# Unread identity products on the matrix engine at four places of a four-layer cross-attention kernel

## The chip, the cores and the metric

The kernel runs on one core of one Trainium2 chip. The metric is the device time of one execution, in microseconds. The engines are PE (TensorE, the matrix engine; its weight loads are listed as PEld), DVE (VectorE), ACT (ScalarE), POOL (GpSimd) and SP (SyncE, which here only issues transfers).

## The reference

Four layers are applied to `x` (16 sequences of 56 tokens, width 256), each with a context of 1,500 keys of width 128 per sequence. Cut to what is computed:

```python
# layer 0, one head over the context, then a gate and a norm
mp = ctx @ W_mem;  a = softmax(x @ mp.T / 16);  mc = a @ mp
x = rmsnorm(x + sigmoid(concat(x, mc) @ W_gate.T + b) * mc)
# layers 1 and 3: 16 heads of 64 over the context, then a feed-forward network
q = layernorm(x) @ Wq / 8;  k, v = split(ctx @ Wkv)
x = x + tanh(g1) * (softmax(mask(q @ k.T)) @ v) @ Wo
x = x + tanh(g2) * gelu(layernorm(x) @ W1) @ W2
# layer 2: causal self-attention with rotary positions (two sets of weights, picked
# per token), then 16 heads of 8 over the context, then a gated MLP
x = x + where(vm, self_attn(rmsnorm(x)) @ v_dense, ... @ l_dense)
x = x + softmax(cq @ ck.T) @ cv @ cdense_w
x = x + where(vm, mlp_v(rmsnorm(x)), mlp_l(rmsnorm(x)))
```

## The kernel before, in words

The program is one hand-ordered instruction list per engine. Engines meet through semaphores: `then_inc` signals, `on.wait_ge` waits and is left out where an earlier wait of the same engine already covers it. PE writes its products into eight PSUM banks; a product of one stage takes the next bank in turn, and `bank_free` waits until that bank's last content was emptied by ACT or DVE. The 896 tokens are 7 tiles of 128, handled as tiles 0 to 3 and 4 to 6 where a norm is computed. An fp32 product is recorded as two MATMUL instructions, a transpose as one; a transpose streams the identity (`ident`) through PE with the data as weights.

Four stages matter here.

- **First attention** (`pe_l0`, layer 0). Eight units of two sequences. Step `s` on PE does the scores of unit `s` (L666), the sums of unit `s-2` (L678, 24 products of 64 columns) and the transposes of the softmax of unit `s-1` (L692, 12 of them), in that order. ACT and DVE copy the transposes out (L702) before the sums of that unit can start. Steps 8 and 9 have no scores left. Then all engines meet (`join`), `pe_l0_gate` makes the 7 products of L768, the 4 of L772 and the 28 of L778, and POOL, after cutting the next query weights (L562, L564), multiplies and adds per tile (L796, L798) for DVE's square sums (L812).
- **First norm** (`pe_transposes` L502 and `pe_queries`). DVE computes two norms in a row for tiles 0 to 3 (from L819 on), PE transposes the rows, ACT scales them out (L557), DVE cuts them into two parts (L562, L564), and the projections of layer 1 start (L582, fp32r, 6 products each; then L875). DVE goes on with the norms of tiles 4 to 6 before it empties the first projection (L618).
- **Self-attention** (`pe_front`). Eight pairs of sequences. Step `s` does, in this order, the turn of tile `s-1` (L1451), queries and keys of tile `s` (L1431), values of pair `s` (L1443), the transposed weights of pair `s-2` (L1474), the scores of pair `s-1` (L1466), the sums of pair `s-2` (L1485) and the output product of tile `s-4` (L1495). From step 7 on tiles are used up, and from step 8 on pairs too, so the work of PE thins out. The weights of a pair wait for DVE's softmax, whose last operation is L1619; it starts from the scores (L1602). Then come a norm (L502) and the queries of the next attention (L1532).
- **Third attention** (`pe_narrow`). 96 slots of scores, and seven slots behind them without scores. Slots 97 to 99 hold only the 12 `fill` calls of the last group of rows, four transposes each (L1799), into two banks in turn, which ACT (L1903) and DVE (L1901) copy out. Then the last sums (L1812), the norm's transposes (L502) and the MLP (L2062).

## Time and profile before

| | |
|---|---|
| runs, us | 2384.64, 2389.21, 4637.36 (median 2389.21) |
| profiled execution, its own time | 2383.55 us |
| its span | 2381.8 us |
| mean granted clock of PE | 0.983 |
| PE busy | 2299.6 us (97% of the span) |
| DVE busy | 1576.9 us (66%) |
| ACT busy | 1289.9 us (54%) |
| POOL busy | 669.4 us (28%) |

One of the three runs, 4637.36 us, is far from the other two and from the profiled execution. The granted clock is a share of PE's full 2.4 GHz: 1.00 is that level, 0.50 is 1.2 GHz, and a value between them in a row means that the stretch holds both. The parts of the profile used below are the share of the chain that ended last, windows (busy time of each engine and the granted clock in chosen stretches) and timelines (instructions in order of time, neighbours of one kind merged; the bracket at the end is the idle time before it and what ended it).

### The profile page before, as it was taken

What the parts mean: (1) busy time and instruction counts of PE and PEld (TensorE: products, weight loads), DVE (VectorE), ACT (ScalarE), POOL (GpSimd) and SP (SyncE); (2) the same over time, 40 slices, a digit from 0 to 9 for tenths busy, and PEclk for the clock granted to TensorE, in tenths of its full rate; (3) what the DMA queues carried; (4) which work ended last, traced back from release to release, by engine and by line L of the source; (5) the groups of instructions that cost most, each with busy time, mean ns of one, the idle gap of its engine ahead of it and who ended that gap; (6) DMA issues with size and microseconds to landing.
All of it is one profiled execution on the core that took longest, in us unless ns stands there. A gap on an engine that the chain in (4) does not pass through costs nothing.

```text
span 2381.8 us, 42122 instructions
## 1 busy us (share of the span) xinstructions
PE 2299.6 (97%) x16416; PEld 1900.5 (80%) x16416; DVE 1576.9 (66%) x4256; ACT 1289.9 (54%) x2204; POOL 669.4 (28%) x752
## 2 busy tenths in 40 slices
PE   6979999999999999789999999999999999999999
PEld 3857999999999895456666666556899999999988
DVE  2256777777777656677777777414777777777764
ACT  1235555555555543267777777412555555555553
POOL 0045343444443224210000000011543434344330
PEclk8889999999999999899999999899999999999999
DMA  8720111111211110010000000310021111111010
GB/s 264 201 93 17 46 43 46 43 48 41 58 31 43 55 36 21 1 53 27 27 27 27 27 14 1 127 36 4 19 58 40 50 45 44 46 43 46 27 54 17
DMA packets 36136, 116.02 MB, mean 49 GB/s; under 512 B 4618, under 2 KB 18546, under 8 KB 35938
## 3 DMA queue, kind: packets, MB, share of 16 engines
q1 hardware_dynamic: 33474, 101.04, 14.0%
q10 hardware_dynamic: 2464, 12.29, 2.0%
q8 instruction: 131, 2.15, 0.4%
q14 instruction: 67, 0.55, 0.1%
HBM read 112.40 MB, written 0.92 MB: 48 GB/s over the span
## 4 chain that ended last, share of the span: by engine, by line
PE 90%; ACT 5%; DVE 3%; DMA 1%; issue 0%; ACTq 0%; SPq 0%; DVEq 0%
PE bank L1051 20%; PE bank L1038 19%; PE bank L1065 12%; PE bank L1799 7%; PE bank L582 7%; PE bank L2062 3%; PE bank L1812 3%; PE bank L1785 3%; ACT n_scores L1911 3%; PE bank L678 2%; PE bank L1759 2%; PE bank L2075 2%; PE bank L875 1%; PE bank L1763 1%; PE bank L1232 1%; PE bank L1077 1%
## 5 line engine op out<-in xcount | busy, mean ns | idle before, releaser
L1101 ACT CAST p_T_high<-bank 125x512 fp32r<-125x512 f32 x672 | 350.6, 595 | 515.9 <-PE bank L1065 515.9
L1158 DVE TENSOR_TENSOR p_T_low<-bank,p_T_high 125x512 fp32r<-125x512 f32 x672 | 422.5, 684 | 258.0 <-ACT p_T_high L1101 258.0
L1124 DVE CUSTOM_DVE_ANT_0 scores<-bank,mask 128x500 f32<-128x500 f32 x672 | 418.4, 672 | 0.8 <-PE bank L1038 0.8
L1111 ACT ACTIVATE scores<-scores,row_max 128x1500 f32<-128x1500 f32 x224 | 353.4, 1578 | 2.7 <-DVE row_max L1129 2.7
L1051 PE MATMUL bank<-p_T_high,keys_nat_high 125*128 125x256 f32 (+1 forms) x1152 | 346.0, 300 | 1.7 <-ACT inverse L1108 1.7
L1051 PE MATMUL bank<-p_T_high,keys_nat_low 125*128 125x256 f32 (+1 forms) x1152 | 346.3, 301 | 0.0
L1051 PE MATMUL bank<-p_T_low,keys_nat_high 125*128 125x256 f32 (+1 forms) x1152 | 346.2, 301 | 0.0
L1065 PE MATMUL bank<-ident,scores 128*125 128x128 f32 x2688 | 331.1, 273 | 2.7 <-ACT scores L1111 2.7
L1065 PEld LDWEIGHTS bank<-ident,scores 128*125 128x125 f32 x2688 | 318.2, 187 | 5.7 <-ACT scores L1111 5.7
L1038 PE MATMUL bank<-keys_T_high,q_stage_high 128*128 128x500 f32 x672 | 280.1, 417 | 0.0
L1946 DVE CUSTOM_DVE_ANT_0 n_scores<-bank,n_zeros 112x500 f32<-112x500 f32 x384 | 236.9, 673 | 56.7 <-PE bank L1785 56.7
L1038 PE MATMUL bank<-keys_T_high,q_stage_low 128*128 128x500 f32 x672 | 261.2, 389 | 0.0
L1038 PE MATMUL bank<-keys_T_low,q_stage_high 128*128 128x500 f32 x672 | 260.7, 388 | 0.0
L1799 PEld LDWEIGHTS bank<-ident,n_scores 112*125 112x125 f32 x1536 | 186.9, 190 | 88.1 <-issue 29.7
L1799 PE MATMUL bank<-ident,n_scores 112*125 112x112 f32 x1536 | 220.2, 287 | 13.4 <-ACT n_p_T L1903 7.3
L1051 PEld LDWEIGHTS bank<-p_T_high,keys_nat_high 125*128 125x128 f32 x1152 | 216.7, 188 | 10.2 <-ACT inverse L1108 2.2
L1051 PEld LDWEIGHTS bank<-p_T_low,keys_nat_high 125*128 125x128 f32 x1152 | 217.0, 188 | 8.5
L1051 PEld LDWEIGHTS bank<-p_T_high,keys_nat_low 125*128 125x128 f32 x1152 | 216.7, 188 | 0.0
L1911 ACT ACTIVATE n_scores<-n_scores,n_stats 112x1500 f32<-112x1500 f32 x128 | 197.8, 1546 | 0.4 <-DVE n_stats L1952 0.4
L1164 POOL CAST q_stage_high<-q_and_o 128x256 fp32r<-128x256 f32 (+1 forms) x96 | 41.7, 434 | 412.8 <-PE bank L1038 412.6
L1038 PEld LDWEIGHTS bank<-keys_T_high,q_stage_low 128*128 128x128 f32 x672 | 126.2, 188 | 26.3
L1038 PEld LDWEIGHTS bank<-keys_T_high,q_stage_high 128*128 128x128 f32 x672 | 126.9, 189 | 19.0 <-issue 1.6
(242 smaller groups left out, 3611.9 us busy)
## 6 DMA issues: line engine op xcount, KB each, us to landing
ctx_T<-in_ctxT SPq DMA_DIRECT2D x32, 750.0 KB, 4.3
ctx_nat<-in_ctx SPq DMA_DIRECT2D x32, 672.0 KB
q_and_o<-in_ctxT SPq DMA_DIRECT2D x16, 750.0 KB, 9.2
n_ctx_T<-in_ctxT SPq DMA_DIRECT2D x16, 750.0 KB, 4.2
q_and_o<-in_ctx ACTq DMA_DIRECT2D x16, 672.0 KB
mask_bytes<-in_mask SPq DMA_DIRECT2D x32, 187.5 KB, 5.2
weights<-in_L_W SPq DMA_DIRECT2D x4, 1024.0 KB, 6.2
ctx_nat<-in_ctx SPq DMA_DIRECT2D x32, 78.0 KB
```

What stands on the lines that cost most here:

```text
L582: x = e.matmul(out, left[i], right[j], start=start and n == 0, stop=stop and n == 2)
L1038: m = e.matmul(psum[c][:, 0:CHK], QSs[i][g % 2][:, lo:lo + 128], KTs[j][b % 2][:, cols], start=(n == 0), stop=(n == 2))
L1051: m = e.matmul(psum[6 + g % 2][:, cols_g], KNs[i][b % 2][0:KP, cols], PTs[j][g % 2][0:KP, k, cols_g], start=(k == 0 and n == 0), stop=(k = ...
L1065: m = e.transpose(psum[3 + c][0:KP, 128 * k:128 * k + 128], SB[u % 2][:, (4 * c + k) * KP:(4 * c + k + 1) * KP], ident)
L1101: e.copy(PTs[0][g % 2][0:KP, 4 * c:4 * c + 4, lo:lo + 128], psum[3 + c][0:KP, :].rearrange("p (k r) -> p k r", k=4)).then_inc(s_eh, 1)
L1111: e.activation(SB[s % 2], SB[s % 2], ACT.Exp, bias=mx[:, s % 4, 3:4], accum_out=mx[:, s % 4, 4:5]).then_inc(s_ex, 1)
L1124: e.tensor_tensor_reduce(out=SB[u % 2][:, c * CHK:(c + 1) * CHK], in0=psum[c][:, 0:CHK], in1=mb[:, c * CHK:(c + 1) * CHK], scale=1.0, scal ...
L1158: e.tensor_tensor(low, psum[3 + c][0:KP, :].rearrange("p (k r) -> p k r", k=4), high.bitcast(F32), ALU.subtract).then_inc(s_el, 1)
L1785: return e.matmul(psum[r][0:PAIR, 0:CHK], n_qs[i][b % 2][rows, PAIR * hh:PAIR * hh + PAIR], CK[j][b % 2][rows, c * CHK:(c + 1) * CHK], sta ...
L1799: m = e.transpose(psum[4 + t % 2][0:KP, PAIR * k:PAIR * k + PAIR], n_unit(quad, r)[0:PAIR, at:at + KP], ident[0:PAIR, 0:PAIR])
L1911: e.activation(unit, unit, ACT.Exp, bias=n_st[0:PAIR, quad % 2, r, 3:4], accum_out=n_st[0:PAIR, quad % 2, r, 4:5]).then_inc(s_n_ex, 1)
L1946: e.tensor_tensor_reduce(out=n_unit(quad, r)[0:PAIR, c * CHK:(c + 1) * CHK], in0=psum[r][0:PAIR, 0:CHK], in1=n_zeros[0:PAIR, :], scale=1.0 ...
```

## The change

A new helper, `pe_fill_in`, multiplies the identity by itself, repeated side by side: 512 columns wide, or 256 with `copies=2`, in plain fp32. It signals nothing, and no engine reads the result. It is called at five spots:

1. In steps 8 and 9 of the first attention, two and one products, ahead of the sums.
2. Ahead of the first transposes of layer 1's norm, eight products, and ahead of the first projection, two.
3. In steps 7, 8 and 9 of the self-attention, two, four and four products, ahead of the pair's transposed weights.
4. In slots 97 to 99 of the third attention, one product of 256 columns behind each `fill`.

DVE, ACT, POOL and SP keep their lists as they were. The waits that come with the products make sure that the bank they write into is free.

```diff
--- before.py
+++ after.py
@@ -494,6 +494,13 @@
                 on.wait_ge(*prod.emptied[prod.ahead[i]])
 
 
+        def pe_fill_in(e, at_bank, times, copies=4):
+
+            for _ in range(times):
+                e.matmul(at_bank[:, 0:128 * copies].rearrange("p (o n) -> p o n", o=copies), ident,
+                         ident.rearrange("p (o n) -> p o n", o=1).to_broadcast([128, copies, 128]),
+                         start=True, stop=True)
+
         def pe_transposes(e, on, n, h):
             for (m, k), i in n.parts[h].items():
                 bank_free(on, i)
@@ -666,6 +673,9 @@
                             x = e.matmul(psum[c][64 * n:64 * n + 64, 0:CHK], q0T_flat[:, PAD * b:PAD * b + PAD],
                                          kt0[b % 4][:, c * CHK:(c + 1) * CHK], start=True, stop=True)
                         x.then_inc(s_sc, 1)
+                if s >= L0U:
+                    on.wait_ge(s_mx, 3 * L0U)
+                    pe_fill_in(e, psum[0], L0U + 2 - s)
                 if s >= 2:
                     u = s - 2
                     on.wait_ge(s_l0_ea, 2 * u + 2)
@@ -1507,6 +1517,9 @@
                     values(s)
                 if s == 0:
                     pe_transposes(e, on, in_norm, 1)
+                if NT <= s < PAIRS + 2:
+                    on.wait_ge(s_rot, 3 * NT)
+                    pe_fill_in(e, front_bank(F_QK), (2, 4, 4)[s - NT])
                 if 2 <= s < PAIRS + 2:
                     weights(s - 2)
                 if 1 <= s <= PAIRS:
@@ -1841,8 +1854,11 @@
                         pe_cd(e, on, t)
                 for half in range(2):
                     if 0 <= quad < QUADS:
-                        fill(quad, ts[2 * half])
-                        fill(quad, ts[2 * half + 1])
+                        for t in ts[2 * half:2 * half + 2]:
+                            fill(quad, t)
+                            if s > SLOTS:
+                                on.wait_ge(*prod.emptied[cd_prod[0]])
+                                pe_fill_in(e, bank(cd_prod[0]), 1, 2)
                     if made:
                         product(*made[half])
                     if b < B:
@@ -2153,7 +2169,11 @@
             pe_q0(e, on)
             pe_l0(e, on)
             pe_l0_gate(e, on)
+            bank_free(on, g1.q_norm.parts[0][0, 0])
+            pe_fill_in(e, bank(g1.q_norm.parts[0][0, 0]), 8)
             pe_transposes(e, on, g1.q_norm, 0)
+            bank_free(on, g1.q[0, 0])
+            pe_fill_in(e, bank(g1.q[0, 0]), 2)
             pe_queries(e, on, g1)
             pe_cross(e, on, layers[0], g1)
             join(e, on, J["l1"])
```

PE at the end of the first attention, steps 8 and 9, before. The names are those of the program: `area` holds the scores, `q_and_o` the keys; the bracket lists the semaphores waited for.

```order
L692 MATMUL bank<-ident,area 125x128 x11
L678 MATMUL bank<-area,q_and_o 128x64 [waits s_o_out,s_l0_keys0,s_l0_evac_dve,s_l0_evac_act]
L678 MATMUL bank<-area,q_and_o 128x64 x11
L678 MATMUL bank<-area,q_and_o 128x64 [waits s_l0_keys1]
L678 MATMUL bank<-area,q_and_o 128x64 x11
L692 MATMUL bank<-ident,area 125x128 [waits s_l0_normed]
L692 MATMUL bank<-ident,area 125x128 x11
L678 MATMUL bank<-area,q_and_o 128x64 [waits s_o_out,s_l0_keys2,s_l0_evac_dve,s_l0_evac_act]
```

And now:

```order
L702 MATMUL bank<-ident,area 125x128 x11
L500 MATMUL bank<-ident 128x512 [waits s_max]
L500 MATMUL bank<-ident 128x512
L688 MATMUL bank<-area,q_and_o 128x64 [waits s_o_out,s_l0_keys0,s_l0_evac_dve,s_l0_evac_act]
L688 MATMUL bank<-area,q_and_o 128x64 x11
L688 MATMUL bank<-area,q_and_o 128x64 [waits s_l0_keys1]
L688 MATMUL bank<-area,q_and_o 128x64 x11
L702 MATMUL bank<-ident,area 125x128 [waits s_l0_normed]
L702 MATMUL bank<-ident,area 125x128 x11
L500 MATMUL bank<-ident 128x512
L688 MATMUL bank<-area,q_and_o 128x64 [waits s_o_out,s_l0_keys2,s_l0_evac_dve,s_l0_evac_act]
```

Two products stand between the transposes and the first sums, one between the next transposes and the last sums; nothing else moved.

PE around the first norm, now; `x_normed` holds the rows to be transposed, `x_T_r` the cut ones. Before, the rows of L500 were not there, and the wait for `s_emptied_dve` stood at the first projection.

```order
L788 MATMUL bank<-weights,x_T 128x256 x15
L500 MATMUL bank<-ident 128x512 x8
L509 MATMUL bank<-ident,x_normed 128x128 [waits s_rows] x4
L509 MATMUL bank<-ident,x_normed 128x128 [waits s_emptied_dve]
L509 MATMUL bank<-ident,x_normed 128x128 x3
L500 MATMUL bank<-ident 128x512 [waits s_emptied_dve]
L500 MATMUL bank<-ident 128x512
L589 MATMUL bank<-x_T_r,weights_r 128x448 [waits s_cut,s_w_l1a,s_weights_cut,s_emptied_act]
```

The eight follow the last gate product without a wait; the other two wait only for a bank that DVE emptied in the gate stage.

PE at slot 97 of the third attention, now; `n_scores` are the softmax rows.

```order
L1825 MATMUL bank<-n_p_T,q_and_o 32x224 x8
L1812 MATMUL bank<-ident,n_scores 125x112 [waits s_n_p_act,s_n_exp]
L1812 MATMUL bank<-ident,n_scores 125x112 x3
L500 MATMUL bank<-ident 128x256 [waits s_emptied_dve]
L1812 MATMUL bank<-ident,n_scores 125x112 [waits s_n_p_dve]
L1812 MATMUL bank<-ident,n_scores 125x112 x3
L500 MATMUL bank<-ident 128x256
L1812 MATMUL bank<-ident,n_scores 125x112 [waits s_n_p_act]
```

Before, the groups of four transposes followed each other directly; now each of the 12 has a product behind it. The first of them waits for the residual of tile 0, for which its bank was last used.

## Rows read from the trace of the kernel before

**Rows 1.** The page, part 4: the chain that ended last, by engine.

```profile
PE 90%; ACT 5%; DVE 3%; DMA 1%; issue 0%; ACTq 0%; SPq 0%; DVEq 0%
```

**Rows 2.** Windows. Stretch, length, busy us (instructions) per engine, PEclk, DMA share, GB/s.

```profile
97.70:108.00 10.30, 10.30 (x50) 10.30 (x50) 0.28 (x1) 0.89 (x2) 0.00 (x0) 0.50 0.52 133
108.00:111.40 3.40, 2.57 (x24) 2.41 (x23) 0.69 (x1) 0.28 (x1) 0.00 (x0) 1.00 0.00 0
111.40:121.60 10.20, 9.79 (x39) 8.88 (x39) 1.55 (x4) 0.20 (x1) 0.00 (x0) 0.50 0.24 74
...
142.10:155.80 13.70, 5.58 (x17) 4.44 (x18) 12.19 (x38) 1.97 (x4) 0.33 (x1) 0.50 0.00 0
...
975.00:978.40 3.40, 3.33 (x12) 2.10 (x14) 0.01 (x1) 1.07 (x2) 3.40 (x4) 0.50 0.02 5
...
1497.20:1510.80 13.60, 12.61 (x74) 10.09 (x74) 5.59 (x20) 8.72 (x16) 0.00 (x0) 0.50 0.67 237
```

**Rows 3.** Timeline, PE, 84 to 142. Start, us, engine, line, idle before it.

```profile
87.87 5.57 PE L678 MATMUL bank<-area,q_and_o 125*128 125x64 f32 x48
93.28 1.53 PE L692 MATMUL bank<-ident,area 128*125 128x128 f32 x12
96.47 9.38 PE L678 MATMUL bank<-area,q_and_o 125*128 125x64 f32 x48 [1.67 <-ACT area L702]
105.65 2.66 PE L692 MATMUL bank<-ident,area 128*125 128x128 f32 x12
109.14 8.44 PE L678 MATMUL bank<-area,q_and_o 125*128 125x64 f32 x48 [0.83 <-ACT area L702]
117.98 5.07 PE L768 MATMUL bank<-weights,q_and_o 128*128 128x256 f32 x14 [0.41 <-DVEq L331]
...
126.79 12.32 PE L778 MATMUL bank<-weights,x_T 128*128 128x256 f32 x56 [0.72 <-ACT x_T L616]
```

**Rows 4.** Timelines, POOL and DVE, of the gate stage.

```profile
131.07 0.73 POOL L796 TENSOR_TENSOR area<-area 128x256 f32<-128x256 f32 x1
...
139.49 0.68 DVE L819 TENSOR_SCALAR row_stats<-row_stats 128x4 f32<-128x4 f32 x1
```

**Rows 5.** Timeline, PE, 144 to 168: first norm and first projections.

```profile
147.69 2.30 PE L502 MATMUL bank<-ident,x_normed 128*128 128x128 f32 x8 [8.58 <-DVE x_normed L524]
152.52 4.16 PE L582 MATMUL bank<-x_T_r,weights_r 128*128 128x448 f32 x12 [2.53 <-DVE x_T_r L564]
158.45 1.02 PE L875 MATMUL bank<-area,weights 64*128 64x448 f32 x4 [1.77 <-DVE area L618]
```

**Rows 6.** Timeline, PE, 954 to 1050: last self-attention pairs.

```profile
964.80 1.09 PE L1474 MATMUL bank<-ident,q_and_o 128*128 128x128 f32 x8
965.83 1.73 PE L1466 MATMUL bank<-q_and_o 128*64 128x448 f32 x8
...
975.07 1.97 PE L1474 MATMUL bank<-ident,q_and_o 128*128 128x128 f32 x8 [2.74 <-DVE q_and_o L1619]
...
986.67 1.97 PE L1474 MATMUL bank<-ident,q_and_o 128*128 128x128 f32 x8 [4.86 <-DVE q_and_o L1619]
988.56 3.26 PE L1466 MATMUL bank<-q_and_o 128*64 128x448 f32 x8
...
1012.98 3.19 PE L1532 MATMUL bank<-x_T,weights 128*128 128x448 f32 x4 [1.01 <-DVE x_T L541]
```

**Rows 7.** Timeline, PE, 1486 to 1517: end of the third attention.

```profile
1495.42 3.09 PE L1799 MATMUL bank<-ident,n_scores 112*125 112x112 f32 x16 [1.72 <-ACT q_and_o L1903]
1498.78 5.75 PE L1799 MATMUL bank<-ident,n_scores 112*125 112x112 f32 x24 [0.27 <-ACT q_and_o L1903]
1505.25 3.22 PE L1812 MATMUL bank<-q_and_o,n_values 125*32 125x224 f32 x32 [0.72 <-DVE q_and_o L1901]
...
1508.54 3.04 PE L502 MATMUL bank<-ident,area 128*128 128x128 f32 x16
1511.51 1.72 PE L1812 MATMUL bank<-q_and_o,n_values 125*32 125x224 f32 x32
```

## The prediction

> **What bounds the kernel now.** I read four views, in this order. The chain of waits first: 90% of the chain that ended last is PE [rows 1]. So a microsecond counts where PE works on the chain, and a wait of PE counts only for what it does to the work behind it. Next the windows, cut where the granted clock changes: PE runs at its low level, 1.2 GHz, in 97.7 to 108.0 and 111.4 to 121.6 (end of the first attention and start of the gate), 142.1 to 155.8 (first norm), a few short stretches from 975 on (last self-attention pairs), and 1497.2 to 1510.8 (end of the third attention) [rows 2]. Each of them comes behind a place where PE waited. These are the five spots of the edit. Third, the timelines of PE there, for what the same instruction takes at either level: 48 instructions of sums take 5.57 us at the high level and 9.38 or 8.44 us at the low one; 12 transposes 1.53 and 2.66 [rows 3]. Last, the other engines there, to see who would be late next.
>
> **What a new product costs.** The 28 gate products of 256 columns, 56 instructions, take 12.32 us at the high level [rows 3]: 0.44 us each. A new product of 512 columns is then 0.88 us, one of 256 columns 0.44 us. At the low level it is twice that: 1.76 and 0.88 us. All of it is PE time; no other engine's list changes, and the new waits are on work long done (the last score maxima, a bank emptied in the gate stage, the last rotation), so I cost them at nothing. The one with something close behind it is the bank of tile 0's residual in slot 97; DVE empties it in the pause that ACT leaves there anyway.
>
> **First attention.** Two products, 1.76 us, stand in a wait of 1.67 us [rows 3]: 0.1 us lost. If the clock stays up, the sums behind them fall from 9.38 to 5.57 us: 3.8 us won. From the start of the next transposes (105.65) to the last sums (109.14) it is 3.49 us. The same distance at the high level is 3.19 us, from 93.28 to 96.47, so at least 0.3 us is won; but there ACT issues key transfers before it copies, which step 9 doesn't. At most the transposes' own 1.13 us is won. I take 1.1, nearer the place itself, since the third product (0.88 us) then just fills the 0.83 us of wait. The last sums: 8.44 to 5.57, 2.9 us. The seven products of L768: 5.07 us against 7 x 0.44 = 3.1, 2.0 us. Not all of that counts. POOL starts the tiles at 131.07, behind its cut of weights whose transfer is issued at the join, so relative to the join it moves not at all [rows 4]. Four tiles at two operations of 0.73 us bring it to about 137, and DVE's square sum and two adds to about 138.3, where it starts the norm at 139.49 today [rows 4]: 1.2 us. Sum: 3.8 + 1.1 + 2.9 + 1.2 - 0.1 = **8.9 us**.
>
> **First norm.** Eight products, 7.0 us, in a wait of 8.58 us; two, 1.8 us, in one of 2.53 us [rows 5]. They cost nothing at the high level. What do they bring? Very little: the transposes wait for DVE's rows, and the 12 projections (4.16 us, mostly low) are followed by a wait for DVE [rows 5], which meanwhile works through the norms of tiles 4 to 6. Faster projections only make the wait of 1.77 us longer, to about 3 us. That wait has no product in it, and it is as long as the one of 2.74 us behind which the clock fell at 975 [rows 2, 6]. From there PE is the bound. A low stretch of 3.4 us, the length in [rows 2], can cost half of that, 1.7 us; two of them 3.4. Between +0.2 (transposes a little earlier) and -3.4 I take **-1.0 us**: one such stretch, more likely than not.
>
> **Last self-attention pairs.** The waits of 2.74 and 4.86 us [rows 6], and a third like the second, get 1.8, 3.5 and 3.5 us of products: hidden. DVE's softmax between them is not shortened, but it starts when PE's transposes and scores are done, so their low clock is on the chain. Second pair: transposes 1.97 against 1.09, scores 3.26 against 1.73 [rows 6]: 2.4 us. First pair: transposes 0.9, of the scores only the beginning is low (the low stretch is 3.4 us long, which caps the gain at 1.7): 1.5 us. Third: its transposes, 0.9, and those of the norm behind them, in part waiting for rows: 1.1, between 0.9 and 1.7. The queries at 1012.98 take 3.19 us, half of it too much [rows 6]; but the small waits ahead of them, 1.01 us the last, stay uncovered, so I take half of 1.6: 0.8. Sum: **5.8 us** (4.5 to 6.7).
>
> **End of the third attention.** Here the products are partly on the chain. The last 24 transposes, six groups, take 5.75 us at the low level, 0.96 us a group [rows 7]. At the high level 12 transposes take 1.53 us [rows 3], so four with 112 columns about 0.4, and the product 0.44: 0.84 a group. 6 x 0.12 = 0.7 us won. Ahead of them ACT's exponentials and copies set the pace (waits of 1.72 and 0.27 us [rows 7]). Then the sums, 3.22 against 1.72 us: 1.5. The norm's 16 transposes, 3.04 us, would take about 2.0: 1.0. Sum: **3.2 us**. If the clock were not low here anyway, the 12 products, 5.3 us, less the waits of 1.72, 0.27 and 0.72, would cost 2.6 us.
>
> **A rule against it.** PE's clock rose at 108.0 [rows 2], and from 105.65 on it had done nothing but 12 transposes, 2.66 us long [rows 3]; they stream the same identity that the new products stream. On the other side 24 transposes from 1498.78 did not raise it [rows 2, 7]. The Trainium skill says in "TensorE: Matmul & The Clock Gate", Part 4 (PE-mode transpose), that in transpose mode the full clock doesn't engage, since it doesn't count as PE being busy in the same way. By that rule the products between transposes have to hold the clock alone. By the first of the two rows the transposes help them; I go by it, and keep the other as a rival.
>
> **The sum.** 8.9 - 1.0 + 5.8 + 3.2 = 16.9 us, against the profiled execution's own 2383.55 us: 2366.6 us. The two runs shown near it are 1.1 and 5.7 us above that execution, so I put the median of the changed kernel 1.9 us higher: **2368.5 us**, 0.9% below the median of 2389.21.
>
> **The rivals.**
> - *Given back (chance 0.22).* The clock falls in waits that no product covers, above all behind the first projections (-3.4), the queries stay slow (5.0 instead of 5.8), and at the end of the third attention the typical execution has little low clock to win back, so that the products show (-2.6). 8.9 - 3.4 + 5.0 - 2.6 = 7.9 us: 2375.7, with the same 1.9 on top 2377.6. For it: clock falls come behind waits of quite different length, so they may not be the same in each execution. Against: the waits with products are the longest ones.
> - *Transposes don't count (0.07).* The end of the third attention stays low: 12 products at 0.88 = 10.6 us less 2.7 of waits cost 7.9 us instead of a gain of 3.2. 16.9 - 11.1 = 5.8 us: 2377.8 us. The rule above is the Trainium skill's form of it. The rise at 108.0 speaks against it.
> - *Slower than before (0.05).* The products don't hold the clock (a product that is mostly zeros is not counted, or too little), and so run at 1.76 us each. They outgrow the waits: 3.5 - 1.7 and 1.8 - 0.8 in the first attention, 14.1 - 8.6 and 3.5 - 2.5 at the norm, 3.5 - 2.7 and twice 7.0 - 4.9 at the pairs, 7.9 at the third attention: 22 us, 2406 us. The eight ahead of the norm decide it: from 8.58 / 8 = 1.07 us each on they delay it. Against: identity was streamed up to 108.0, and the clock rose.
> - *Forecast (0.66).* All four places keep the high clock, 2361 to 2374 us.
>
> **The numbers.** The time is the forecast's. The range goes from 2360 us (first attention 9, pairs 6.7, third attention 4, norm +0.2, and executions like the profiled one) to 2381 us, which takes in both rivals at 2378 and a median like the slower of the two runs. About 1 in 8 is left out, mostly the slower case. All cases lie within 2% of 2389.21 (2341 to 2437), about what a measurement of this kernel can tell from no change: 0.98 within, 0.01 on either side.
>
> **What would show it.** Windows of the changed kernel: clock 1.00 through the first attention's end and the gate, the sums 5.6 us each, the join 7.7 us earlier; DVE's norm start about 9 us earlier; the wait ahead of the products of L875 about 3 us, and perhaps a low stretch behind it; the distance between two pairs' transposes 10.3 us, as from 964.80 to 975.07, instead of 11.6 [rows 6]; groups of 0.84 us in slots 98 and 99, sums of 1.7 us behind them. The forecast is wrong if a product takes 1.76 us in one of the waits, if the copies of step 9 still take 3.2 us, or if sums follow with the clock at 0.50 all the same.

## The result

The changed kernel takes **2376.77 us** (median, 2369.47 to 2382.78), the kernel before 2385.01 us in the same comparison: ratio 0.9966, 95% interval 0.9954 to 0.9978, that is 8 us less (5 to 11). Measured again on the chip of the last mends, beside 2384.66 us of before, it took 2372.58 us: 0.9952 (0.9935 to 0.9969), 11 us less. Over all 22 executions its median is 2375.9 us. The direction, the range and the class (within 2%) were forecast; the gain was put at 16.9 us, and half to two thirds of it came.

The profiled execution of the changed kernel has a time of 2373.76 us and a span of 2372.0 us, 9.8 us less than before. Its windows, cut where the granted clock changes (columns as in [rows 2]), show what was promised and one thing that was not:

```profile
98.40:105.20 6.80, 6.80 (x33) 6.80 (x33) 0.27 (x1) 0.74 (x2) 0.00 (x0) 0.50 0.28 80
105.20:142.70 37.50, 34.10 (x157) 24.76 (x156) 16.56 (x49) 9.13 (x18) 16.88 (x18) 1.00 0.47 143
142.70:146.10 3.40, 3.40 (x6) 1.19 (x5) 2.82 (x9) 1.14 (x3) 0.00 (x0) 0.50 0.00 0
969.60:1002.90 33.30, 27.15 (x187) 13.33 (x188) 22.40 (x46) 7.85 (x14) 4.30 (x5) 1.00 0.00 0
1030.20:1043.90 13.70, 13.70 (x77) 10.66 (x76) 7.09 (x21) 8.70 (x15) 1.59 (x3) 0.50 0.00 1
1480.20:1506.60 26.40, 25.30 (x251) 19.68 (x250) 11.37 (x34) 15.46 (x28) 0.00 (x0) 1.00 0.47 162
```

Against [rows 2], the pairs (969.60) and the end of the third attention (1480.20) are now without any low clock. But the clock is still at 0.50 from 98.40, though for 6.8 us instead of 10.3; again at 142.70; and, new, for 13.7 us from 1030.20 on, inside the third attention. Before had there only the short low stretch (a stretch with the clock at 0.50) that begins 9.2 us into that stage, and the changed kernel has one like it, 3.4 us from 1016.5 on. The row of before:

```profile
1026.20:1029.60 3.40, 3.40 (x12) 1.33 (x5) 2.48 (x8) 0.52 (x1) 0.00 (x0) 0.50 0.00 0
```

The timeline of PE at the end of the first attention (start, us, instruction, idle before it) answers [rows 3]:

```profile
92.42 1.88 PE L500 MATMUL bank<-ident 128*128 128x512 f32 x4
94.25 2.89 PE L688 MATMUL bank<-area,q_and_o 125*128 125x64 f32 x24
98.06 5.14 PE L688 MATMUL bank<-area,q_and_o 125*128 125x64 f32 x24 [0.92 <-DMA q_and_o<-in_ctx]
103.00 2.60 PE L702 MATMUL bank<-ident,area 128*125 128x128 f32 x12
105.43 1.02 PE L500 MATMUL bank<-ident 128*128 128x512 f32 x2
106.42 5.54 PE L688 MATMUL bank<-area,q_and_o 125*128 125x64 f32 x48
112.38 3.29 PE L778 MATMUL bank<-weights,q_and_o 128*128 128x256 f32 x14 [0.41 <-DVEq L331]
```

The two products (92.42) fill the wait for ACT as planned, 1.88 us in four instructions. Half-way through unit 6's sums PE then waits 0.92 us, but for DMA: the keys. The clock falls right behind it, at 98.40; the second 24 sums take 5.14 us, the first 24 took 2.89, and the transposes take 2.60 (2.66 in [rows 3]). From these transposes to the last sums it is 3.42 us, hardly less than the 3.49 of before. Only the last sums (106.42) are as forecast, 5.54 us instead of 8.44. The gate starts at 112.38, 5.6 us earlier, where 7.7 were expected.

The first norm, for [rows 5]:

```profile
131.56 7.03 PE L500 MATMUL bank<-ident 128*128 128x512 f32 x16
140.85 1.74 PE L509 MATMUL bank<-ident,x_normed 128*128 128x128 f32 x8 [2.26 <-DVE x_normed L531]
142.42 3.32 PE L500 MATMUL bank<-ident 128*128 128x512 f32 x4
145.58 2.94 PE L589 MATMUL bank<-x_T_r,weights_r 128*128 128x448 f32 x12
151.47 1.02 PE L885 MATMUL bank<-area,weights 64*128 64x448 f32 x4 [2.95 <-DVE area L625]
152.42 2.16 PE L589 MATMUL bank<-x_T_r,weights_r 128*128 128x448 f32 x6
154.51 1.87 PE L885 MATMUL bank<-area,weights 64*128 64x448 f32 x4
156.31 1.51 PE L589 MATMUL bank<-x_T_r,weights_r 128*128 128x448 f32 x6
```

Eight products take 7.03 us: 0.88 us each, the price of the forecast. The two behind the transposes take 3.32 us, 1.66 each, for the clock is low there, from 142.70 on. It costs nothing here: from the transposes to the projections it is 4.73 us, against 4.83 in [rows 5]. The wait ahead of L885 (L875 before) grew from 1.77 to 2.95 us, as forecast, and part of what follows is low: 2.16 us for six projections that take 1.51 at 156.31.

The pairs and queries, for [rows 6], and the place of the new loss, on PE:

```profile
969.59 1.09 PE L1484 MATMUL bank<-ident,q_and_o 128*128 128x128 f32 x8 [0.83 <-DVE q_and_o L1632]
970.61 1.72 PE L1476 MATMUL bank<-q_and_o 128*64 128x448 f32 x8
...
974.61 3.60 PE L500 MATMUL bank<-ident 128*128 128x512 f32 x8
979.63 1.09 PE L1484 MATMUL bank<-ident,q_and_o 128*128 128x128 f32 x8 [1.42 <-DVE q_and_o L1632]
...
989.68 1.09 PE L1484 MATMUL bank<-ident,q_and_o 128*128 128x128 f32 x8 [1.42 <-DVE q_and_o L1632]
...
1002.55 3.00 PE L1545 MATMUL bank<-x_T,weights 128*128 128x448 f32 x4 [1.01 <-DVE x_T L548]
1006.31 2.78 PE L1772 MATMUL bank<-n_ctx_T,value_weights 128*128 128x500 f32 x6 [0.77 <-DVEq L331]
```

```profile
1029.95 1.82 PE L1812 MATMUL bank<-ident,n_scores 112*125 112x112 f32 x8 [1.60 <-ACT n_p_T L1919]
```

From pair to pair it is 10.04 us, 10.3 were forecast, and scores take 1.72 us. The queries at 1002.55 are still slow, 3.00 us. In slot 4 of the third attention PE waits 1.60 us for ACT's copies of the transposed weights, and the low 13.7 us start there.

The end of the third attention, for [rows 7]:

```profile
1488.69 0.69 PE L1812 MATMUL bank<-ident,n_scores 112*125 112x112 f32 x4 [0.83 <-ACT q_and_o L1919]
...
1492.28 0.59 PE L1812 MATMUL bank<-ident,n_scores 112*125 112x112 f32 x4
...
1493.15 0.59 PE L1812 MATMUL bank<-ident,n_scores 112*125 112x112 f32 x4
...
1497.95 1.72 PE L1825 MATMUL bank<-q_and_o,n_values 125*32 125x224 f32 x32 [0.27 <-DVE q_and_o L1917]
...
1499.70 2.03 PE L509 MATMUL bank<-ident,area 128*128 128x128 f32 x16
...
1506.60 3.65 PE L2078 MATMUL bank<-x_T,weights 128*128 128x448 f32 x9
```

A group takes 0.87 us (1492.28 to 1493.15), 0.84 forecast; sums 1.72 and the norm's transposes 2.03 us, as forecast.

**Where the microseconds are.** One execution says little about a clock that falls at different waits each time. So here are means over the profiles of three executions of before and four of the changed kernel, between the same instructions on PE (us):

```
stretch                               step said   before  changed  gained
start to sums of unit 6                  -0.1      96.1     95.3     0.9
sums of unit 6 to sums of unit 7         +4.9      13.2     13.0     0.2
sums of unit 7 to the gate's first       +2.9      10.2      6.0     4.2
gate to first absorbed queries           +1.2      40.7     39.2     1.5
from there to the first pair             -1.0     764.5    766.3    -1.8
first five pairs                          0        52.1     52.1     0.0
last three pairs, norm, queries          +5.8      41.4     36.5     5.0
third attention up to its last slots      0       471.7    475.4    -3.7
end of the third attention               +3.2      29.3     26.4     3.0
the rest                                  0       865.4    865.4     0.0
sum                                      16.9    2384.7   2375.6     9.1
```

Two lines hold the missing 8 us: the sums of unit 6, and the third attention.

### The profile page after: what moved, and what is told of

Read it like the earlier page. It is cut to its first block, busy times and chain, and to the rows that moved or that the text cites. A ratio compares the mean times of both kernels' runs of the same rounds, so it can differ in the third digit from the quotient of the medians.

```text
span 2372.0 us, 42261 instructions
## 1 busy us (share of the span) xinstructions
PE 2309.4 (97%) x16486; PEld 1901.8 (80%) x16486; DVE 1576.2 (66%) x4256; ACT 1288.7 (54%) x2204; POOL 668.8 (28%) x752
## 3 DMA queue, kind: packets, MB, share of 16 engines
q8 instruction: 132, 2.16, 0.4%
## 4 chain that ended last, share of the span: by engine, by line
PE 89%; ACT 5%; DVE 3%; DMA 2%; POOL 0%; issue 0%; ACTq 0%; SPq 0%; DVEq 0%; POOLq 0%
PE bank L1061 20%; PE bank L1048 19%; PE bank L1075 12%; PE bank L1812 8%; PE bank L589 7%; PE bank L2078 3%; PE bank L1825 3%; PE bank L1798 3%; ACT n_scores L1927 2%; PE bank L1772 2%; PE bank L2091 2%; PE bank L688 2%; PE bank L885 1%; PE bank L1776 1%; PE bank L1242 1%; PE bank L1087 1%
## 5 line engine op out<-in xcount | busy, mean ns | idle before, releaser
L1061 PEld LDWEIGHTS bank<-p_T_high,keys_nat_high 125*128 125x128 f32 x1152 | 216.7, 188 | 10.2 <-ACT inverse L1118 2.2
```

The lines of the kernel that those rows point to most:

```text
L1061: m = e.matmul(psum[6 + g % 2][:, cols_g], KNs[i][b % 2][0:KP, cols], PTs[j][g % 2][0:KP, k, cols_g], start=(k == 0 and n == 0), stop=(k = ...
```

## The experiments

**One piece at a time.** Each kernel is the changed one with three of its four pieces taken out; for example the one that keeps the first attention:

```diff
-                if NT <= s < PAIRS + 2:
-                    on.wait_ge(s_rot, 3 * NT)
-                    pe_fill_in(e, front_bank(F_QK), (2, 4, 4)[s - NT])
...
-                            if s > SLOTS:
-                                on.wait_ge(*prod.emptied[cd_prod[0]])
-                                pe_fill_in(e, bank(cd_prod[0]), 1, 2)
...
-            pe_fill_in(e, bank(g1.q_norm.parts[0][0, 0]), 8)
...
-            pe_fill_in(e, bank(g1.q[0, 0]), 2)
```

> Only the three products at the end of the first attention stay. Theory 1 (the profiled execution of before had more low clock than a usual one, so the sum was made too large): 4 to 7 us faster than before; the sums behind the first two products partly wait for keys that are still in transfer. Rival (the sizes by place were right, and the gain is lost again in low stretches elsewhere that the change brings): 8.9 us faster, and the granted clock of the profile is 1.00 from 94 us to the join.

> Only the ten products around the first norm stay. Both theories: 0 to 2 us slower than before, no gain. The norm's chain on VectorE is as long as before, the wait behind the first 12 projections grows from 1.8 to about 3 us, and in most executions the clock falls behind it. If instead it is 2 us or more faster, the projections' low clock was on the chain and my step was wrong.

> Only the ten products at the last self-attention pairs stay. Theory 1: 4 to 5 us faster, from the distances between the transposes of two pairs (10.0 us each in place of 11.6 and 12.4). Rival: 5.8 us faster in the stretch. Both: at least as much as the other places together, if theory 1 holds.

> Only the twelve products at the end of the third attention stay. Theory 1: within 1 us of before, since a usual execution of before has less low clock there and the products themselves stand on the chain (12 x 0.44 us less the waits). Rival: 3.2 us faster, as the two profiles show it (3.1 us).

Measured, as ratios to before: first attention alone 0.9982 (0.9972 to 0.9993), 4.3 us; norm alone 1.0001 (0.9991 to 1.001), nothing; pairs alone 0.9981 (0.9971 to 0.9991), 4.5 us; end of the third attention alone 0.998 (0.997 to 0.9991), 4.8 us. The first three came as their theories said. The pieces add up to 13.6 us, each with some 2.5 us of uncertainty; that this is more than the 8 to 11 us that they give together is likely, but not clear of these errors. For the third attention the rival was right: from the first products behind it to the next stage it takes 28.9 to 29.6 us in the six executions without the products, and 26.3 to 26.4 in every one with them. The kernel with the pairs alone gives the pairs' 5 us in full (35.5 us instead of 41.4) and loses them: its third attention takes 475.2 us instead of 469.8.

The profiled execution of the first piece alone was the fastest of its eleven (2370.85 us against a median of 2380.18): its keys came in time and its sums took 7.8 us. In the one with the end of the third attention alone they didn't (PE; start, us, instruction, idle):

```profile
96.80 4.06 PE L685 MATMUL bank<-area,q_and_o 125*128 125x64 f32 x24 [1.98 <-DMA q_and_o<-in_ctx]
101.94 5.39 PE L685 MATMUL bank<-area,q_and_o 125*128 125x64 f32 x24 [1.07 <-DMA q_and_o<-in_ctx]
```

Two waits, 1.98 and 1.07 us, both for keys from DMA. In [rows 3] the wait ahead of the same sums is for ACT.

**The same kernels again**, to see whether low stretches move from one execution to the next:

> The kernel before, once more, for a second profile. Theory 1: its low stretches lie elsewhere or are shorter than in the first profile, above all at the end of the third attention (there 13.6 us) and the end of the first attention (20.5 us in all). Rival: they are the same as in the first profile.

> The kernel before a third time. Expectation as for the second: by theory 1 the low stretches move from execution to execution, by the rival they do not.

> The changed kernel once more, for a second profile. Theory 1: the places with products have no low clock, or little; a low stretch of some 10 us turns up or not at places without products (start of the third attention, queries, first projections), as it does in before. Rival: the low stretch at the start of the third attention (13.6 us in the first profile, 3.4 us in before) is there again, since the change causes it.

> The changed kernel a third time. Expectation as for the second profile: by theory 1 the low stretch at the start of the third attention comes and goes, by the rival it stays.

Single executions: before 2391.27 and 2384.55 us, changed 2373.05 and 2380.69 us. PE waits for keys in or ahead of unit 6's sums for 1.81 and 2.05 us in the two of before, and for 0.62 and 1.65 us in the two of the changed kernel. The execution on which the forecast was built is the one of three without such a wait. Theory 1 had expected less low clock in the other executions of before. There was more: 27.3 us in one piece from 97.7 on and 30.7 from 95.3 on, against 20.4 in two pieces, and again 13.7 us at the end of the third attention in both. The rival was right on the third attention: its low stretch is there in both of the changed kernel (13.7 and 17.1 us long), and in one of before. In that one the third attention begins at 1019.87, and two low stretches lie in it:

```profile
1029.60:1033.00 3.40, 3.40 (x5) 1.12 (x4) 3.01 (x9) 0.58 (x1) 0.00 (x0) 0.50 0.00 0
1043.20:1060.30 17.10, 16.77 (x86) 13.23 (x87) 9.90 (x31) 11.53 (x19) 1.59 (x3) 0.50 0.01 5
```

**Mend one: one product in slot 4**, where PE waits 1.60 us:

```diff
+                    if s == 4 and half == 0:
+                        on.wait_ge(*n_prod_out(1, 5))
+                        pe_fill_in(e, psum[6], 1)
```

> The changed kernel with one more product of 512 columns (0.88 us at the high level) in the third attention, slot 4, where PE waits 1.60 us for ACT and the clock then falls for 13.7 us. Theory (the 3.8 us lost in the third attention are that one low stretch, and it starts because PE waits there just behind the shorter pairs): the stretch is gone, the third attention takes 469.8 us again instead of 474 to 475.3 (from the first product of its prologue to the products behind it), and the time is 3.5 to 4.5 us below the changed kernel's, about 12 us below the kernel before: 2372 to 2374 against 2385. Rival (the clock falls there whatever a single wait does, or falls at the next wait instead): 474 to 475 us again, a low stretch of over 10 us within 30 us of that place, and the time of the changed kernel, 2376 to 2378.

Measured: 2372.91 us, 0.9952 (0.9936 to 0.9969). The low stretch behind slot 4 is gone. The third attention took 471.45 us, between what both expected: the clock was low for 6.8 us near its beginning, from 1015.2 on. The time is also what the changed kernel took when it was measured again (0.9952), so that by itself it tells nothing of the mend's worth; the same holds for the next one.

**Mend two: keys first.** The transfers for the gate stage are issued only behind the products of values of unit L0U-2:

```diff
             w = s_w["l0b"]
+            on.wait_ge(s_pv, L0U - 2)
             e.dma_start(w_memT
```

> The changed kernel, but the transfers for the gate stage are issued later (behind unit L0U-2's products of values instead of before), so that the keys of units 6 and 7 of the first attention have the DMA queues more to themselves. Theory (the first attention gained 2 to 5 us less than forecast because half-way through the sums of unit 6 PE waited 0.92 us for keys, and the clock fell there): the stretch from the sums of unit 6 to those of unit 7 takes 7.8 us instead of 11.8 to 14.1, no low stretch near 98 us, the join 3 to 4 us earlier; if the gate's weights then come late, up to 2 us of it is lost again: 1 to 4 us below the changed kernel. Rival (the fall near 98 us is not the wait's doing, or the keys come no earlier): 11 to 14 us again, no difference, or slower by the late weights.

Measured: 2371.11 us, 0.995 (0.9935 to 0.9964). No wait for DMA, 7.77 us from sums to sums; the wait of 0.57 us left there is for ACT (last sums at 103.91):

```profile
96.14 5.57 PE L688 MATMUL bank<-area,q_and_o 125*128 125x64 f32 x48 [0.57 <-ACT area L712]
...
103.91 5.54 PE L688 MATMUL bank<-area,q_and_o 125*128 125x64 f32 x48
```

**Without the norm's ten products:**

```diff
-            bank_free(on, g1.q_norm.parts[0][0, 0])
-            pe_fill_in(e, bank(g1.q_norm.parts[0][0, 0]), 8)
             pe_transposes(e, on, g1.q_norm, 0)
-            bank_free(on, g1.q[0, 0])
-            pe_fill_in(e, bank(g1.q[0, 0]), 2)
```

> The changed kernel without the ten products at the first norm. Theory (they only make the clock fall later, in the stretch where PE is the bound): from the first projections behind the norm (L875 before) to the first self-attention pair it takes 764.4 us in every run instead of 764.5 to 767.3, and up to there nothing is slower: 0 to 2 us below the changed kernel, 1.5 taken. Rival (the products hold the clock in the norm and its projections, worth the forecast's +0.2 at least and more as the gate ends earlier now): 0 to 2 us slower than the changed kernel.

Measured: 2372.32 us, 0.9953 (0.9938 to 0.9968), no different from the changed kernel's 0.9952 and 0.9966. My theory of why failed in its profile: behind the absorbed queries it took 767.7 us, more than with the products. The clock was low for 23.9 us from 129.4 on, through the norm and past it:

```profile
136.02 2.30 PE L509 MATMUL bank<-ident,x_normed 128*128 128x128 f32 x8 [8.79 <-DVE x_normed L531]
140.85 4.82 PE L589 MATMUL bank<-x_T_r,weights_r 128*128 128x448 f32 x12 [2.53 <-DVE x_T_r L571]
146.79 1.87 PE L885 MATMUL bank<-area,weights 64*128 64x448 f32 x4 [1.12 <-DVE area L625]
```

**Transposes instead of products:**

```diff
-                e.matmul(at_bank[:, 0:128 * copies]...
+                for k in range(2 * copies):
+                    e.transpose(at_bank[:, 128 * (k % copies):128 * (k % copies) + 128], ident, ident)
```

> The changed kernel, with each new product of 512 columns made of eight transposes of the identity instead (of 256 columns: four). Theory by the rows (transposes stream columns like products and hold the clock as well): low stretches as in the changed kernel, no new ones in the pairs or at the end of the third attention, 36 to 37 us for the last three pairs and 26.4 us at the end of the third attention, time within 2 us of the changed kernel's if eight transposes take about as long as one product (they are more instructions, so up to 5 us more at the places on the chain). Rival (transposes do not count as work of PE): the pairs take 41 us and the end of the third attention 29 or more, as without products, the first norm ends low, and the time is that of the kernel before or more, 2385 to 2395.

Measured: 2376.93 us, 0.9968 (0.9957 to 0.998), like the changed kernel. Eight transposes take as long as one product: 16 in 1.91 us, where two products take 1.88. And the clock stays at 1.00 through all three places (timeline, then windows). At the third, from 1487.25 to the sums at 1496.43, PE runs nothing but transposes:

```profile
92.78 1.91 PE L501 MATMUL bank<-ident 128*128 128x128 f32 x16
...
97.74 2.89 PE L687 MATMUL bank<-area,q_and_o 125*128 125x64 f32 x24 [0.24 <-DMA q_and_o<-in_ctx]
...
101.84 1.04 PE L501 MATMUL bank<-ident 128*128 128x128 f32 x8
```

```profile
94.00:109.00 15.00, 14.34 (x124) 13.74 (x123) 1.24 (x3) 1.84 (x5) 0.00 (x0) 1.00 0.51 124
966.60:999.80 33.20, 27.13 (x235) 17.36 (x236) 22.41 (x46) 7.86 (x14) 4.34 (x5) 1.00 0.00 1
1478.80:1505.00 26.20, 25.07 (x274) 20.42 (x273) 11.37 (x34) 15.42 (x28) 0.00 (x0) 1.00 0.48 163
```

**Mend three: three products ahead of the absorbed queries**, alone, then two mends, then all three, beside the changed kernel:

```diff
+                    if g.l == 1 and (j, half, hh) == (0, 0, 0):
+                        pe_fill_in(e, bank(i), 3)
                     on.wait_ge(*prod.emptied[g.q[j, half]])
```

> The changed kernel with three more products of 512 columns (2.6 us) in the wait of 2.95 us ahead of the first products of the absorbed queries (L885), behind which PE is the bound. Theory (up to 3.3 us are lost from there to the first self-attention pair because the clock is low behind that wait, which grew as the stretches ahead of it became faster): from that place to the first pair it takes 764.4 to 764.8 us instead of 764.5 to 767.7 (767.3, 767.3 and 767.7 in three of the seven kernels with products in the first attention), 1 to 3 us below the changed kernel. Rival (a low stretch that begins before the wait, at 129 to 147 us, goes on through it whatever PE does, so that the three products take 5.3 us and delay the absorbed queries): 766 to 769 us, 0 to 2 us slower than the changed kernel.

> The changed kernel with two of the mends at once: keys of units 6 and 7 ahead of the gate's transfers, and one product in the third attention's slot 4. Theory (the waits are separate causes, and each is worth its own stretch): sums of unit 6 to those of unit 7 in 7.8 us, third attention in 469.8 to 471.5 us, 5 to 7 us below the changed kernel: 2369 to 2371 us, 0.994 of the kernel before. Rival (the chip takes the high clock away at some other wait instead, so that gains do not add): 2371 to 2373 us, no better than either mend alone (2371.1 and 2372.9).

> The changed kernel with all three mends: keys ahead, one product in slot 4, three products ahead of the absorbed queries. Theory: 6 to 9 us below the changed kernel, 2367 to 2370 us, that is the forecast's 2368.5 us at last, 0.993 of the kernel before; low stretches only ahead of 40 us, one of 3 to 7 us at the first norm, and two or three in the norm behind the pairs. Rival (gains do not add, or the three products are run low): 2371 to 2374 us.

> The changed kernel again, beside its mended forms on the same chip. Theory: 0.9966 of the kernel before, 2376 to 2378 us, a low stretch of 6 to 10 us near 100 us if PE waits half a microsecond or more for keys there, and one of 13 to 17 us 24 us into the third attention if its grid falls behind the wait for ACT there. Rival (what was measured first was partly another chip's or day's): 2371 to 2374 us, like the kernels without one piece of it, and then the mends are worth nothing.

Measured: mend three alone 2373.11 us, 0.9953 (0.9939 to 0.9966); mends one and two 2371.3 us, 0.9942 (0.9929 to 0.9954); all three **2366.59 us, 0.9923 (0.9912 to 0.9935)**; the changed kernel 2372.58 us, 0.9952 (0.9935 to 0.9969). Two mends together came out where the rival had them: 2371.3 us is no less than mend two alone, 2371.11, though both stretches are short in its profile (7.76 and 469.9 us). Mend three does its part (764.49 us behind it, against 767.38 in the changed kernel's profile), but its profiled execution lost 8.7 us in the third attention, and its time shows nothing. The changed kernel's time is the one that the rival named (2371 to 2374 us), though its profile has both low stretches of the theory, 10.2 us from 98.5 and 17.1 us from 1037.2 on; its two ratios, 0.9966 and 0.9952, overlap in their intervals. So no mend alone is told from the changed kernel by its time; all three together are, narrowly. With all three, the windows and the two places on PE:

```profile
98.94:106.71 7.77, 7.77 (x63) 7.00 (x63) 0.96 (x2) 1.07 (x2) 0.00 (x0) 1.00 1.06 254
106.71:141.60 34.89, 31.03 (x143) 23.10 (x142) 13.87 (x40) 8.18 (x16) 16.88 (x18) 1.00 0.54 175
152.43:916.90 764.47, 759.75 (x5034) 686.26 (x5034) 538.35 (x1443) 417.07 (x716) 299.95 (x330) 1.00 0.14 41
1006.07:1475.93 469.86, 458.11 (x4590) 320.24 (x4590) 354.30 (x1043) 367.72 (x621) 25.91 (x49) 1.00 0.08 26
```

```profile
149.14 2.74 PE L500 MATMUL bank<-ident 128*128 128x512 f32 x6
152.43 1.02 PE L888 MATMUL bank<-area,weights 64*128 64x448 f32 x4 [0.55 <-DVE area L625]
```

```profile
1028.28 1.04 PE L500 MATMUL bank<-ident 128*128 128x512 f32 x2
1029.69 1.18 PE L1815 MATMUL bank<-ident,n_scores 112*125 112x112 f32 x8 [0.38 <-ACT n_p_T L1925]
```

**All three again, and without the norm's products:**

> The changed kernel with all three mends (keys ahead, slot 4, three products ahead of the absorbed queries), without the ten products at the first norm. Theory (the ten products move nothing that is on the chain, since PE waits there for DVE whatever its clock): within 1.5 us of the kernel with all three mends, gate to absorbed queries 38.9 to 39.8 us, from there to the first pair 764.4 to 764.8 us. Rival (without them the clock falls for over 20 us from about 129 on, as in the one execution seen without them, and the three products ahead of the absorbed queries run at the low level): 766 to 769 us from there to the first pair, 2 to 4 us slower than with them.

> The kernel with all three mends again, beside the one without the norm's products. Theory (three separate waits, three separate losses): 0.992 to 0.9935 of the kernel before, 2366 to 2369 us; sums of unit 6 in 7.8 us, third attention 469.9 us, 764.5 us behind the absorbed queries. Rival (the first measurement, 5 executions, was lucky): 0.9945 or more, 2371 us or more, with a low stretch of 13 us or more in one of the three places.

Measured: again 2365.88 us, 0.9923 (0.9899 to 0.9946); without the norm's products 2367.27 us, 0.9933 (0.991 to 0.9957). The eleven executions of the mended kernel lie between 2364.7 and 2369.7 us; the 22 of the changed kernel between 2366.4 and 2382.8. Whether the ten products at the norm are worth anything stays open: without them it took 40.3 us from gate to absorbed queries against 38.8 with them, but 38.9 in the earlier kernel without them, and the times don't tell the two apart.

What each mend does to its stretch, over all profiles:

```
stretch (us)                  without the mend                        with it
sums of unit 6 to unit 7      11.8 to 14.1 in five of nine with the   7.8 in five of five
                              products, 7.8 to 8.4 in four
absorbed queries to pair 1    764.4 to 767.7 in ten with products in  764.5 in four of four
                              the first attention
third attention               473.9 to 478.7 in eight of nine with    469.9 to 471.5 in five of five
                              products in the pairs, 469.9 in one
                              (without those: 469.8 to 470.0 in
                              five of six, 475.4 in one)
```

## Why the prediction was wrong

**First attention, +8.9: 6.8 came.** The steps for the last sums, L768 and the gate held (5.7 us against 2.9 + 1.2; more than forecast, since two of the three executions of before were low there for longer, 10.9 us against 8.8 in the profiled one). The step that failed is the first: "the sums behind them fall from 9.38 to 5.57" and, hanging on it, the transposes' 1.1. They were put at 4.9 us together and brought 0.2. I took the wait ahead of the sums for ACT's because the one profiled execution has it so. In four of the five other executions without products in the first attention (b2, b3, norm alone, third attention alone) PE waits for keys in or ahead of these sums, 1.8 to 2.5 us, and in the four of the changed kernel 0.6 to 1.7 us; no product ahead of the sums covers a wait in their middle. The nine executions with the products and the transfers as they were show the wait's weight: 11.8 to 14.1 us for this stretch in the five in which PE waited 0.62 us or more for keys, 7.8 to 8.4 us in the four in which it waited 0.39 us or less. With keys first it is 7.8 us in all five profiles. That is 4.9 us less than the 12.67 us of the profile that the forecast was built on, so the size was right for keys that come in time. A part is lost ahead of it, where the sums of unit 6 start later (96.8 us on average against 95.3): the gate starts at 110.6 us, against 114.2 in the changed kernel and 119.6 in before, so that 9.0 us are won up to there instead of 5.3.

**First norm, -1.0: -1.8.** Mechanism and place were right (a wait of 2.95 us, low clock behind it). The size was a guess between two cases, and over all profiles both occur. With the norm's products (or transposes in their place) and nothing in the wait ahead of the absorbed queries, that wait is 2.19 to 3.22 us long, and seven of nine executions lost 1.5 to 2.9 us behind it. Without the norm's products it is 1.11 to 1.77 us, and six of seven lost nothing. The seventh (the changed kernel without the norm's products, a wait of 1.12 us) lost 3.3 us in a low stretch that had begun at 129.4 already, so that faster projections are not the only way to this loss. Three products in the wait bring it to zero in four of four.

**Last pairs, +5.8: 5.0**, within its own range. Between pairs it was better than forecast, 10.04 us. The 0.8 us of the queries came in one of the four profiles only (35.5 us from the first of these pairs to the third attention, against 36.7 to 37.0).

**Third attention, a step that the sum lacks: -3.7.** I treated the pairs' gain as final once it was made. But PE waits 1.24 to 1.65 us in slot 4, some 24 us into the third attention, and has no product there. With the products in the pairs, the clock fell at that wait in eight of nine executions; without them, in one of six. With one product in that wait it stayed up in five of five. Whether it is the shorter pairs that make the fall likelier is not shown, and the profiles have a sign that divides them better. Every execution has a low stretch that begins 8.6 to 10.6 us into the third attention, ahead of slot 4. Without a product in slot 4, the clock fell there in all nine executions in which that stretch began at 9.7 us or later, and in none of the six in which it began at 9.5 us or earlier; the one execution without products in the pairs that fell, and the one with them that didn't, are each on the right side. Of the five with a product in slot 4 only two are of the first kind (9.9 and 10.5 us), so that only these two test it; the other three might have kept the clock without it. The length of the wait doesn't divide them: it is 1.25 us in the profile of before, where nothing fell, and 1.24 us in one of the changed kernel, where it did.

**End of the third attention, +3.2: 3.0.** Right in each of its three terms. The case in which the clock isn't low here anyway, which would have cost 2.6 us, was seen in no execution.

**The rivals.** "Given back" named the time within 1 us (2377.6 us), in part by luck, and half of its mechanism holds: waits without a product lower the clock again, and behind the first projections 1.8 us were lost of its 3.4. But it also looked for a loss at the end of the third attention, which gained in every execution, and not at the keys or in slot 4. "Transposes don't count" is refuted, though its 2377.8 us are as near (with the 1.9 us that the other sums add they would be 2379.7): with transposes in place of all new products the clock stays at 1.00 in the three windows above, in one of them through 9 us of nothing but transposes, and the time is the same. That is shown for holding the clock; in before, 24 transposes at the low level did not raise it [rows 2, 7]. The Trainium skill's rule in "TensorE: Matmul & The Clock Gate", Part 4 (PE-mode transpose), that the full clock doesn't engage for them, does not hold in this kernel. "Slower" is refuted by 16 instructions in 7.03 us; the 1.66 us each of the two products behind the norm's transposes are the only ones in this profile near its 1.76, and they stood in a wait.

The Trainium skill describes on the same page, under "HAM oscillation — how this bites in real kernels", how a wait for DMA between products throttles PE again. The trace agrees in kind, but not in size: the waits that the page draws are of 3 to 5 us, and here the clock fell behind one of 0.92 us (behind 0.62 us in another execution). I had not asked where else in this kernel such a wait could come up.

The forecast's 2368.5 us is within 3 us of what the products and the three mends give together (2365.9 and 2366.6 us). That is no proof of its sum, for the mended kernel also moves transfers and wins 9.0 us up to the gate, where the sum had 7.7. But the price of a product at the high clock (0.88 us) and the worth of that clock at each place were right; the error was in the list of waits.

## What to carry to other kernels

Where the clock is what one gains, list every wait of PE from about half a microsecond on, also behind the places that are improved, and read it in several executions: a product holds the clock in its own wait, and the next uncovered one can still lower it. A wait on a transfer varies between executions, so the releaser that one profile names may be another's on the next run. And measure the pieces alone as well: here they gave 13.6 us one by one and 8 to 11 together, which hints at a loss outside their places, though the errors of the five numbers nearly cover the difference. Where executions differ, also compare what each had just before the place: only a few profiles with a mend may be of the kind that needed it.

## What the runs showed of the hardware

A fall of the clock costs quite different amounts. From 98.40 on PE was busy for 6.80 of 6.80 us at the low level, and the clock then rose; from 1030.20 on it was busy for 13.70 of 13.70 us before it did, in a stretch of 112-column transposes and products of 32 rows.

The same wait lowers the clock in one execution and not in the next: that of slot 4 was 1.26 us long in the kernel with the pairs alone, where the clock fell, and 1.25 us in the one with keys first, where it didn't. The short low stretch ahead of it had begun 9.7 us into the third attention in the first and 9.3 us in the second. The changed kernel's 22 executions lie up to 16 us apart; the eleven with the three waits covered, 5 us.
